# Last feed-forward layer of a decoder: two float32r parts in place of three bf16 parts

## The reference, cut to what matters

```python
def _L3_ffn_ref(x, k0, k1, k2, s0, s1, s2):
    def _conn_dense(kernel_bool, x):
        w = jnp.where(kernel_bool, jnp.float32(1.0), jnp.float32(-1.0))
        return x @ w
    h = jnp.concatenate([x, -x], axis=-1)          # 512 features
    h = jax.nn.relu(s0 * _conn_dense(k0, h)) * 2   # 1024
    h = jax.nn.relu(s1 * _conn_dense(k1, h)) * 2   # 1024
    return s2 * _conn_dense(k2, h)                 # 256
x = _layernorm(x + _L3_ffn_ref(x, ...), axis=-1)   # all in float32
```

## Time and profile before

| | |
|---|---|
| median of 3 runs | 2705.63 us (2703.59 to 2707.63) |
| the profiled execution's span | 2706.3 us |
| last layer, from its first copy to the end | 2431.9 to 2706.3 us |
| TensorE busy, whole span | 2221.0 us, 82% |
| VectorE, ScalarE, GpSimd busy | 1522.7, 941.7, 829.3 us |

### The profile page before, as it was taken

The page is one execution under the profiler, slowest core; times in us unless marked ns, Lnnn a source line. Parts: engine busy times, 40 slices in busy tenths (PEclk is TensorE's granted clock), DMA queues, the critical chain, the costliest instruction groups (busy, mean ns, idle before and its releaser), DMA issues. The chain is left out here.

```text
span 2706.3 us, 38599 instructions
## 1 busy us (share of the span) xinstructions
PE 2221.0 (82%) x14591; PEld 1469.3 (54%) x14591; DVE 1522.7 (56%) x3033; ACT 941.7 (35%) x1543; POOL 829.3 (31%) x614
## 2 busy tenths in 40 slices
PE   7978848895796783897878868989999997779998
PEld 5765534563695672796446635853434343254554
DVE  3784773457333567011734534346999989845553
ACT  3323322231111342232423320125766574424331
POOL 1121221214102202001140004024897989623221
PEclk8989978997897886898889979999999999979999
DMA  4217010001895101896000013653011010010000
GB/s 157 71 40 246 13 46 18 1 2 45 303 377 203 47 16 45 327 360 220 10 24 1 2 57 109 179 171 94 24 39 35 29 44 20 1 51 1 9 9 16
DMA packets 104584, 234.31 MB, mean 87 GB/s; under 512 B 10000, under 2 KB 77456, under 8 KB 95440
## 3 DMA queue, kind: packets, MB, share of 16 engines
q1 hardware_dynamic: 95664, 209.81, 22.3%
q0 software_dynamic: 7680, 20.98, 2.4%
q10 hardware_dynamic: 1056, 1.05, 0.1%
HBM read 175.83 MB, written 55.97 MB: 86 GB/s over the span
## 5 line engine op out<-in xcount | busy, mean ns | idle before, releaser
L3617 POOL TENSOR_TENSOR l_attn_ring<-l_attn_ring,l_attn_c_rows 128x1024 f32<-128x1024 f32 x128 | 302.0, 2359 | 85.7 <-DVE l_attn_ring L3506 85.7
L3506 DVE TENSOR_TENSOR_SCAN l_attn_ring<-bank,l_attn_ring 128x512 f32<-128x512 f32 x256 | 299.1, 1210 | 22.6 <-ACT bank L3392 18.1
L3236 PE MATMUL bank<-l_attn_ring,identity 128*128 128x512 f32 x512 | 251.1, 614 | 37.1 <-POOL l_attn_ring L3617 30.2
L163 PE MATMUL bank<-x_features,weights 128*128 128x512 f32 x544 | 256.2, 617 | 14.6 <-ACT l_attn_silu_z L3306 4.9
L3392 ACT ACTIVATE bank<-l_attn_step,l_attn_minus_exp_a_log 128x508 f32<-128x508 f32 x256 | 173.6, 685 | 161.9 <-DVE l_attn_ring L3506 161.4
L163 PEld LDWEIGHTS bank<-x_features,weights 128*128 128x128 f32 x544 | 104.9, 197 | 140.0 <-issue 121.2
L3236 PEld LDWEIGHTS bank<-l_attn_ring,identity 128*128 128x128 f32 x512 | 96.0, 195 | 151.8 <-issue 104.9
L457 DVE TENSOR_REDUCE negmax_slots<-bank 128x16 f32<-128x2048 f32 x48 | 109.8, 2287 | 102.0 <-PE bank L349 101.6
L3904 PE MATMUL bank<-l_ffn_hidden_parts,l_ffn_sign_weights 128*128 128x512 bf16 x768 | 166.4, 379 | 0.0
L3500 DVE TENSOR_TENSOR l_attn_ring<-l_attn_step_times_input,bank 128x1024 f32<-128x1024 f32 x128 | 153.3, 1198 | 3.6 <-PE bank L3222 1.8
L3904 PEld LDWEIGHTS bank<-l_ffn_hidden_parts,l_ffn_sign_weights 128*128 128x128 bf16 x768 | 75.1, 98 | 90.0
(11 more groups left out here) (680 smaller groups left out, 4558.8 us busy)
## 6 DMA issues: line engine op xcount, KB each, us to landing
l_attn_tile_weights<-l_ffn_experts SPq DMA_DIRECT2D x22, 2180.0 KB, 10.1
ffn_experts_tile_weights<-l_ffn_experts_experts SPq DMA_DIRECT2D x37, 1024.0 KB, 8.6
expert_slots<-zeros SPq DMA_DIRECT2D x8, 2048.0 KB, 13.5
l_attn_c_rows<-state_outputs SPq DMA_DIRECT2D x64, 256.0 KB, 3.2
l_ffn_tile_weights<-l_ffn_experts SPq DMA_DIRECT2D x23, 512.0 KB, 4.5
expert_slots<-residual_sum SPq DMA_DIRECT2D x62, 128.0 KB, 8.7
expert_slots<-zeros SPq DMA_DIRECT2D x1, 5888.0 KB, 27.8
l_ffn_tile_x<-expert_slots SPq DMA_DIRECT2D x23, 256.0 KB, 4.1
```

The lines of the kernel that those rows point to most:

```text
L163: mm = pe.matmul(out, w[:, f, m * P:(m + 1) * P], src[:, f, :], start=start and f == 0, stop=stop and f == k - 1)
L3236: mm = pe.matmul(net.banks[SUMS[j]][:], net.ident[:], ring[n % 4][:, j, :], start=s == 0, stop=s == STATES - 1)
L3506: nc.vector.tensor_tensor_scan(ring[n % 4][:, j, :], net.banks[DECAY[j]][:], ring[n % 4][:, j, :], 0.0, ALU.mult, ALU.add).then_inc(state_ ...
L3617: tt(ring[n % 4][:], ring[n % 4][:], c_row[:, n % STATES, :].unsqueeze(1).broadcast_to([P, 2, T]), ALU.mult).then_inc(out_ready, 1)
```

## The change

Signs and activations of the last layer become float32r, a four-byte type. Each fp32 activation is the sum of two float32r parts, high and low, not of three bf16 parts. So every product has two matmuls in place of three. ScalarE makes `full` and the high part both from PSUM, each with a Relu; VectorE subtracts once; GpSimd has no work left, and w2 is made on VectorE at tile 8. VectorE makes w0 before it splits the first group's x. The first product uses the banks in the order 0, 1, 4, 5, 6, 7, 2, 3; the second product keeps 4 to 7, 0 to 3. A bank is free when the high part is made. The second half of `second` has the output tile as the outer loop. `second` waits for tile 5 of the first product, `third` for tile 1 (before: 5) of the next group's first product. `full` lies in the room of other weights. To make place, the two context buffers are given back before this layer.

```diff
-    def __init__(self, room):
-        self.high, self.middle, self.low = room
-        self.each = room
+    def __init__(self, high, low):
+        self.high, self.low = high, low
+        self.each = (high, low)
...
-        def bank(m):
-            return net.banks[(m + 4) % 8]
+        BANKS = ((0, 1, 4, 5, 6, 7, 2, 3), (4, 5, 6, 7, 0, 1, 2, 3))
+        def bank(layer, m):
+            return net.banks[BANKS[layer][m]]
...
                 def first(g):
                     pe.wait_ge(x_high, g + 1)
-                    pe.wait_ge(x_middle, g + 1)
                     pe.wait_ge(x_low, g + 1)
                     for m in range(8):
-                        free(tile(0, g, m))
+                        if g:
+                            pe.wait_ge(high_ready, tile(1, g - 1, BANKS[1].index(BANKS[0][m])) + 1)
...
                 def second(g):
-                    for half_ in range(2):
-                        if half_ == 1 and g:
-                            pe.wait_ge(finish.var_ready, g)
-                        free(tile(1, g, 4 * half_ + 3))
+                    pe.wait_ge(high_ready, tile(0, g, 5) + 1)
+                    for k in range(8):
+                        if g == 0:
+                            pe.wait_ge(w1_ready, k + 1)
+                        pe.wait_ge(low_ready, tile(0, g, k) + 1)
+                        for m in range(4):
+                            weight_tile(k, m)
+                    if g:
+                        pe.wait_ge(finish.var_ready, g)
+                    for m in range(4, 8):
                         for k in range(8):
...
+                            weight_tile(k, m)
                 def third(g):
-                    pe.wait_ge(full_ready, (tile(0, g + 1, 5) if g + 1 < GROUPS else tile(1, g, 5)) + 1)
+                    pe.wait_ge(high_ready, (tile(0, g + 1, 1) if g + 1 < GROUPS else tile(1, g, 5)) + 1)
...
-                    nc.scalar.activation(full[n % 3][:], bank(m)[:], ACT.Relu,
-                                         scale=scale[:, n // 8 % 2:n // 8 % 2 + 1]).then_inc(full_ready, 1)
-                    act.wait_ge(full_ready, n + 1)
-                    nc.scalar.copy(h.high[:, m, :], full[n % 3][:]).then_inc(high_ready, 1)
+                    by = scale[:, n // 8 % 2:n // 8 % 2 + 1]
+                    nc.scalar.activation(full[n % 3], bank(n // 8 % 2, m)[:], ACT.Relu, scale=by).then_inc(full_ready, 1)
+                    nc.scalar.activation(h.high[:, m, :], bank(n // 8 % 2, m)[:], ACT.Relu, scale=by).then_inc(high_ready, 1)
...
+                dve.wait_ge(net.ready["l3_ffn"], 16)
+                nc.vector.tensor_tensor(w0, k0[:, 0:2, :], k0[:, 2:4, :], ALU.subtract).then_inc(w0_ready, 1)
                 split_x(0)
...
-                    remainder(n)
+                    low(n)
                     if n < 8:
                         nc.vector.tensor_scalar(w1[:, n, :], k1[:, n, :], 2.0, -1.0, ALU.mult,
                                                 ALU.add).then_inc(w1_ready, 1)
-                    if n % 8:
-                        low(n - 1)
-                    if n % 8 == 7:
-                        low(n)
+                    if n == 8:
+                        nc.vector.tensor_scalar(w2, k2, 2.0, -1.0, ALU.mult, ALU.add).then_inc(w2_ready, 1)
...
-            @block.gpsimd
-            def _(pool):
-                for n in range(LAST):
-                    h, m = tile_of(n)
-                    pool.wait_ge(rest_ready, n + 1)
-                    nc.gpsimd.tensor_copy(h.middle[:, m, :], rest[n % 3][:]).then_inc(middle_ready, 1)
-                    if n == 7:
-                        pool.wait_ge(net.ready["l3_ffn"], 16)
-                        nc.gpsimd.tensor_scalar(w2, k2, 2.0, -1.0, ALU.mult, ALU.add).then_inc(w2_ready, 1)
...
-        run(SUBLAYERS[9:])
+        run(SUBLAYERS[9:11])
+        mid.close()
+        run(SUBLAYERS[11:])
```

More of the change, by code:

```diff
@@ L7 @@
 BF16 = mybir.dt.bfloat16
+F32R = mybir.dt.float32r
 I32 = mybir.dt.int32
@@ L98, in __init__ @@
         self.w_room = [sb(f"weights{i}", [P, n]) for i, n in enumerate(cols["room"])]
+        self.ctx_room = [mid.enter_context(nc.sbuf_tensor(f"ctx_tokens{i}", [P, NB, D], F32)) for i in range(2)]
         self.psum = cx.enter_context(nc.psum_tensor("bank", [P, 8, 512], F32))
@@ L3835, in l3_ffn @@
         scale = sb("scales", [P, 2])
[L3836 to L3844, removed]
+        w0, w1, w2 = (sb(f"sign_weights{i}", shape, F32R)[:] for i, shape in enumerate(
+            ([P, FT, 1024], [P, 8, 1024], [P, 8, D])))
+        xs = Parts(*(sb(f"x_{n}", [P, FT, T], F32R)[:] for n in ("high", "low")))
+        h0 = Parts(*(sb(f"hidden0_{n}", [P, 8, T], F32R)[:] for n in ("high", "low")))
+        h1 = Parts(*(sb(f"hidden1_{n}", [P, 8, T], F32R)[:] for n in ("high", "low")))
+        spare = net.w_room[1 - PLACES["l3_ffn"][0]]
+        full = [spare[:, i * T:(i + 1) * T] for i in range(3)]
         bits = w["bits"].bitcast(U8)
         k0, k1, k2 = tiles(bits[:, 0:4096], 4), tiles(bits[:, 4096:4096 + 8192], 8), tiles(bits[:, 4096 + 8192:BITS], 8)
-        (w0_ready, w1_ready, w2_ready, scale_ready, h_in_psum, y_ready, x_high, x_rest_ready, x_middle, x_low,
-         full_ready, high_ready, rest_ready, middle_ready, low_ready, dve_steps) = net.signals(20)[4:]
+        (w0_ready, w1_ready, w2_ready, scale_ready, h_in_psum, y_ready, x_high, x_low,
+         full_ready, high_ready, low_ready, dve_steps) = net.signals(16)[4:]
         finish = Finish(net, net.signals(4))
@@ L3886, in first @@
                         for k in range(FT):
                             for i, part in enumerate(xs.each):
-                                mm = pe.matmul(bank(m)[:], w0[:, k, m * P:(m + 1) * P], part[:, k, :],
-                                               start=k == 0 and i == 0, stop=k == FT - 1 and i == 2)
+                                mm = pe.matmul(bank(0, m)[:], w0[:, k, m * P:(m + 1) * P], part[:, k, :],
+                                               start=k == 0 and i == 0, stop=k == FT - 1 and i == 1)
@@ L3890, in first, with weight_tile @@
+                        mm.then_inc(h_in_psum, 1)
+                def weight_tile(k, m):
+                    for i, part in enumerate(h0.each):
+                        mm = pe.matmul(bank(1, m)[:], w1[:, k, m * P:(m + 1) * P], part[:, k, :],
+                                       start=k == 0 and i == 0, stop=k == 7 and i == 1)
+                    if k == 7:
                         mm.then_inc(h_in_psum, 1)
                 def second(g):
-                    for half_ in range(2):
-                        if half_ == 1 and g:
-                            pe.wait_ge(finish.var_ready, g)
-                        free(tile(1, g, 4 * half_ + 3))
-                        for k in range(8):
[L3898 to L3907, removed]
@@ L3914, in third @@
                                 pe.wait_ge(low_ready, tile(1, g, k) + 1)
-                                pe.wait_ge(middle_ready, tile(1, g, k) + 1)
                             for i, part in enumerate(h1.each):
                                 mm = pe.matmul(half(net, Y, b), part[:, k, seq(b)], w2[:, k, :],
-                                               start=k == 0 and i == 0, stop=k == 7 and i == 2)
+                                               start=k == 0 and i == 0, stop=k == 7 and i == 1)
                         mm.then_inc(y_ready, 1)
@@ L3935, in split_x @@
                         act.wait_ge(h_in_psum, tile(0, g - 1, 7) + 1)
-                    nc.scalar.copy(xs.high[:], net.xT_all[:, g, :, :]).then_inc(x_high, 1)
-                    act.wait_ge(x_rest_ready, g + 1)
-                    nc.scalar.copy(xs.middle[:], x_rest[:]).then_inc(x_middle, 1)
+                    nc.scalar.copy(xs.high, net.xT_all[:, g, :, :]).then_inc(x_high, 1)
                 split_x(0)
@@ L3964, in split_x, with low @@
                     dve.wait_ge(x_high, g + 1)
[L3965 to L3974, removed]
+                    nc.vector.tensor_tensor(xs.low, net.xT_all[:, g, :, :], xs.high,
+                                            ALU.subtract).then_inc(x_low, 1)
+                def low(n):
                     h, m = tile_of(n)
```

22 lines of the change are left out of this document (5 added, 17 removed).

## The result

The changed kernel takes 2620.39 us (median of 4 runs, 2616.27 to 2626.38), the kernel before 2705.57 (also 4 runs): the ratio is 0.9692, 95% interval [0.9676, 0.9708], so 85 us or 3.1% less. The forecast was 2613 us, within 2603 to 2643.

The account below looks back on a forecast made before the run. TensorE's matmuls in the last layer were taken as the bound. Gains of 55.2, 10.4 and 10.7 us (products), 4.8 (start), 2.4 (waits) and 9.0 (end) sum to 92.5, taking 2706.3 to 2613.8; forecast 2613 us, range 2603 to 2643.

Parts of the forecast that it names:

- One sweep a float32r matmul: In the last layer's three products, a float32r matmul needs one sweep, as bf16; forecast 2613 us, chance 0.78.
- rival C: Last layer's matmuls run at half speed, 0.430 us at 512 columns and 0.216 at 256: 2776 us, chance 0.09.
- D: Last layer's float32r matmuls run as fp32, two records, 0.860 us at 512 columns: 3107 us, chance 0.02.
- Its size: Last layer's matmuls cost 0.2158 us at 512 columns, 0.111 at 256; gains of 55.2, 10.4 and 10.7 us.
- The weight load hidden: In all three products of the last layer, four-byte weight loads hide beside the array's work and cost nothing.
- rivals B: Third product waits for its four-byte weights, 0.216 us a 256-column matmul: 26.9 us more, 2640 us, chance 0.08.
- E: Every weight load in line with its matmul, 0.111 us more on each of 896: 2712 us, chance 0.03.
- The start: Last layer's start: first matmul at 2435.5 us, group 0's second product 10.4 us later; 4.8 us gained.
- The waits in the steady groups: Between products of the last layer's groups no wait is left; three stalls before third products go, 2.4 us.
- The end: After the last second product, third-product matmuls end 7.8 us later, for 16.8 before: 9.0 us gained, clock not falling.
- Outside the layer nothing: Outside the last layer only a buffer's place in memory changes: 0 us.

Follow-up runs that it names:

- experiment 8: Changed kernel with plain fp32 in place of float32r, two parts kept, the low one zero: 3110.36 us (one run).
- Experiment 1: Changed kernel with bf16 in place of float32r, still two parts, same instructions and waits: 2611.92 us, ratio 0.9654 to the kernel before.
- 3: Changed kernel with each matmul of the second product cut into two of 256 columns: 2629.82 us (one run).
- experiment 9: Changed kernel with each weight load of the second product cut from 128 to 64 columns, half the output features left out: 2622.74 us (one run).
- experiment 5: Kernel before, three bf16 parts kept, with only the second product's second half reordered to one output tile after another: 2701.14 us, ratio 0.9986.
- 11: Changed kernel with the low parts left out and the one remaining part rounded to bf16: 2527.14 us, ratio 0.9347 to the kernel before.
- experiments 2: Changed kernel with the second half of the second product in the old loop order, input block outside: 2626.68 us, ratio 0.9704 to the kernel before.
- experiment 4: Changed kernel with each matmul of the second product cut into four of 128 columns: 2733.59 us (one run).

## Why the prediction was right, step by step

- *One sweep a float32r matmul* (the forecast, 0.78): right. 128 matmuls take 29.04 us; rival C's 0.430 and D's 0.860 are what fp32 records and matmuls take (experiment 8), not float32r. The Trainium skill gives four passes to true fp32 and has reduced-precision fp32 read four bytes and truncate them (FP8 and Floating Point Precision, TensorE Precision Notes); one sweep for float32r, which no row of before had shown, fits this.
- *Its size*: the term that was mis-sized. I took bf16's 0.2158 and 0.111; measured are 0.2269 and 0.1198. 640 × 0.0111 + 256 × 0.0088 = 9.4 us, and that is the miss of the layer (191.1 − 181.9 = 9.2). The reason that I gave, that the sweeps cost and not the four bytes, was wrong by these 5%. Experiment 1 shows that the type alone makes it (9.4 us of layer), 3 that it is fixed and not by column, 9 that the load's length isn't it. The 0.111 was itself a little high: bf16 takes 0.1092 at 256 columns in experiments 1, 5 and 11, where no wait stands in the way. The whole missed by less than the layer, 7.4 us, because the layer happened to begin earlier (by 3.1 us in the profiled executions); that part is luck. The value that I took was the lower end of my bounds, and the forecast's own range (2606 to 2624, which held the result) had no term for anything between the ends.
- *The weight load hidden*: right as far as rivals B (0.216 in the third) and E (0.111 more on each matmul) go, which did not come; a load every 0.1198 us goes. Whether the added 11 and 9 ns are the load's is open, so "at nothing" is not shown. The Trainium skill gives a load its columns over 1.2 GHz (TensorE: Matmul & The Clock Gate, section LDWEIGHTS), an estimate of 107 ns for 128. The recorded loads last longer, 188 ns, and 134 for 64 columns (experiment 9), but the difference, 54 ns for 64 columns, agrees with it, and the floor of 0.1116 lies just above it.
- *The start*: first matmul 3.58 us after the layer's begin (forecast 3.6), second(0) 10.23 us later (10.4). ScalarE's turn was 1.14, a little under my lower bound of 1.16: two starts from PSUM can be 0.57 apart. Part of the agreement is luck: with the clock's earlier rise of experiments 2, 3 and 9 the same code gives 9.5 for the 10.4.
- *The waits in the steady groups*: right, none is left. The three of before were 2.4 us.
- *The end*: 2612.29 − 2603.87 = 8.4 us for the forecast 7.8 and 16.8 before; 2.15 us to the last 50 matmuls as forecast (2.2); these take 6.27 for 5.6, most of it the pitch. The clock did not fall, as forecast: 1.00 over the last 50.
- *Outside the layer nothing*: no instruction differs, and the layer's start moved by 3.1 us, within what it wanders.
- Where the gain of 83.3 us comes from: second products 165.8 − 116.5 = 49.3, first of groups 1 to 3 9.3, third of groups 0 to 2 8.9, start 2.2 + 2.7, waits 2.4, end 8.4; sum 83.2. So 67.5 of it is the smaller number of matmuls at their new price, in these products; 15.7 is the start, the waits and the end. Of the end's 8.4, about 1.4 is the clock: the last 75 matmuls took 9.82 us before and 8.38 in experiment 5. Experiments 2 and 5 put the loop order of the second half at 3.8 us in the new kernel and 7.2 in the old.

## What to carry to other kernels

Where the chain is one engine from end to end, count its instructions and price each by its pitch (a chain's piece over its count); two parts for three take away a third of it, here of 192 × 0.2158 us, and the new type gave back 5% of what was left. A new type's price is the one number to measure alone, by changing the type and nothing else. And let the last tiles of a product end one after another where another engine must empty them.

## What the runs showed of the hardware that was not expected

- A float32r matmul with its load costs some 13.5 ns beyond 2.4 columns per ns, at 512 and at 256 columns (0.2269, 0.1200), bf16 2.5 ns at both (0.2158, 0.1092). At the low clock it costs the same as bf16: in the first product of both kernels a matmul starts 0.427 us after the one ahead. What it is stays open, the matmul or a fixed part of its load: a load of 64 in place of 128 columns did not lower it (0.2299).
- float32r and bf16 matmuls in turn cost 0.230 each in the mean, more than either type by itself (0.2269, 0.2158).
- The same first product has its second product begin 9.5 or 10.2 us after its first matmul, as the granted clock goes from 0.50 to 1.00 after 3.1 or 5.2 us (experiments 2, 3 and 9; the changed kernel and experiment 4).
- Writing four-byte float32r from one-byte signs takes VectorE as long as writing bf16 (688 and 681 ns for 1024 columns).
